# Products of the identity in two of TensorE's gaps, in a four-layer kernel

## The reference, cut to what matters

```
L0_attn: Q, K, V, gate = x @ W;  scores = (Q K^T) * decay;  Y = scores V;  normalise per head;  (silu(gate) * Y) @ W_O
L0_ffn:  y = x @ (quantised kernel + a b) + bias
L1_attn: retention in chunks of 64 tokens, 4 heads, a gate, W_o
L1_ffn:  route the top 256 of 512 tokens through gelu(x W1 + b1) W2 + b2, weighted by sigmoid(score)
```

## Time and profile before

| what | us |
|---|---|
| median of 3 runs | 806.22 |
| lowest, highest | 803.87, 809.37 |
| the profiled execution, its own time | 807.99 |
| its span, first to last instruction | 805.8 |
| TensorE busy in the span | 757.8 (94%) |
| VectorE, ScalarE, GpSimd busy | 665.8, 424.5, 475.3 |
| mean granted clock of TensorE | 0.977 |

### The profile page before, as it was taken

One profiled execution on the slowest core, in us unless ns is written; L12 is line 12 of the kernel. 1 busy time (PEld: TensorE's weight loads), 2 busy tenths in 40 slices (PEclk: granted clock), 3 DMA queues, 4 the chain that ended last, 5 costly groups with the idle time before them and its releaser, 6 DMA issues.

```text
span 805.8 us, 29577 instructions
## 1 busy us (share of the span) xinstructions
PE 757.8 (94%) x13001; PEld 614.8 (76%) x13001; DVE 665.8 (83%) x1825; ACT 424.5 (53%) x875; POOL 475.3 (59%) x375
## 2 busy tenths in 40 slices
PE   5778999999999999998999999999999999999875
PEld 4666888787887787776878888877888888878653
DVE  6686888888888999997858889987777988888887
ACT  2333555565555565654554446655544565564745
POOL 4467888887888888876543444444434344453544
PEclk9996999999999999999999999999999999999988
DMA  7000100011111110010000000000000000000113
GB/s 229 30 28 29 29 28 16 16 28 29 29 28 30 28 29 2 3 55 3 1 2 2 3 3 2 2 2 2 3 2 2 3 2 2 3 2 16 55 39 105
DMA packets 23284, 18.57 MB, mean 23 GB/s; under 512 B 2146, under 2 KB 20468, under 8 KB 22900
## 3 DMA queue, kind: packets, MB, share of 16 engines
q1 hardware_dynamic: 22596, 16.40, 7.0%
q10 hardware_dynamic: 560, 0.28, 0.1%
HBM read 12.48 MB, written 4.19 MB: 21 GB/s over the span
## 4 chain that ended last, share of the span: by engine, by line
PE 75%; DVE 17%; POOL 3%; ACT 2%; issue 1%; DMA 0%; DVEq 0%; POOLq 0%; ACTq 0%
PE ps L286 20%; PE ps L410 11%; PE ps L401 10%; PE ps L281 5%; PE ps L675 4%; PE ps L364 3%; PE ps L308 3%; PE ps L297 3%; PE ps L384 3%; PE ps L394 2%; POOL grstd L1067 2%; PE ps L356 2%; DVE x L1225 2%; PE ps L667 2%; PE ps L320 2%; PE ps L685 2%
## 5 line engine op out<-in xcount | busy, mean ns | idle before, releaser
L1067 POOL TENSOR_TENSOR grstd<-gve,mhalf 128x32 f32<-128x32 f32 (+1 forms) x32 | 159.0, 4968 | 26.5 <-DVE gve L1280 26.5
L410 PEld LDWEIGHTS ps<-w_s,hid 128*128 128x128 f32 x1024 | 123.5, 192 | 9.0 <-issue 8.0
L410 PE MATMUL ps<-w_s,hid 128*128 128x128 f32 x1024 | 129.0, 277 | 0.7 <-issue 0.7
L401 PE MATMUL ps<-xt_r,w_s 128*128 128x512 f32 x256 | 126.7, 617 | 0.7 <-ACT xt_r L822 0.7
L826 ACT ACTIVATE hid<-ps,b_s 128x512 f32<-128x512 f32 x128 | 84.0, 726 | 24.0 <-PE ps L401 23.8
L1063 POOL TENSOR_TENSOR r_ret<-ve_ret,powers 128x8 f32<-128x8 f32 x32 | 57.8, 1807 | 27.6 <-DVE ve_ret L1211 27.6
L286 PE MATMUL ps<-w_qkvg,xt_p 128*128 128x128 f32 x512 | 71.2, 285 | 2.8 <-ACT xt_p L822 2.8
L1073 POOL TENSOR_TENSOR um<-um 128x96 f32<-128x96 f32 (+1 forms) x32 | 21.3, 665 | 88.5 <-DVE um L1259 88.5
L401 PEld LDWEIGHTS ps<-xt_r,w_s 128*128 128x128 f32 x256 | 45.2, 192 | 35.1 <-issue 30.1
L1058 POOL TENSOR_TENSOR rstd_ln_mod<-ve_ln_mod,mhalf 128x4 f32<-128x4 f32 x32 | 32.3, 1010 | 65.3 <-DVE ve_ln_mod L1211 65.3
L1253 DVE TENSOR_TENSOR sc<-ps,tri 128x1024 f32<-128x1024 f32 (+1 forms) x64 | 58.3, 953 | 15.1 <-PE ps L320 7.6
(11 more groups left out here) (236 smaller groups left out, 1749.8 us busy)
## 6 DMA issues: line engine op xcount, KB each, us to landing
xtin<-in_xt SPq DMA_DIRECT2D x16, 256.0 KB, 3.8
out_x<-base SPq DMA_DIRECT2D x16, 256.0 KB, 2.3
xin<-in_x SPq DMA_DIRECT2D x15, 256.0 KB, 3.0
rot<-in_rot SPq DMA_DIRECT2D x2, 1024.0 KB, 5.9
w_s<-in_w SPq DMA_DIRECT2D x2, 256.0 KB
xin<-in_x ACTq DMA_DIRECT2D x1, 256.0 KB, 4.0
w_qkvg<-in_wqkvg SPq DMA_DIRECT2D x1, 256.0 KB, 3.8
w_qkv<-in_wqkv SPq DMA_DIRECT2D x1, 256.0 KB
```

What stands on the lines that cost most here:

```text
L401: nc.tensor.matmul(bank(k), w1_s[:, f, :], xt["r"][:].rearrange("p j n -> p (j n)"), start=True, stop=True).then_inc(s[f"h{f}"], 1)
L410: mm = nc.tensor.matmul(bank(k, j * P, P), hid[:, f, j * P:(j + 1) * P], w2_s[:, f, :], start=False, stop=(f == last and j == NT - 1), ski ...
L1067: nc.gpsimd.tensor_tensor(grstd[:, 0:n], gve[:, 0:n], mhalf[:, 0:n], ALU.pow) \
```

## The change

A helper `keep_busy(times, k)` issues `times` products of the identity with itself into bank k. It is called in two places of TensorE's program: five products into bank 2 in slot g = -1, behind the gate product of batch 0 and ahead of the wait for `qkr`; and 18 products into bank 6 (X1) in `slot_end`, behind `transpose_y` and ahead of the wait for `ln_mod_xn`. One line is indented further, inside the same `if`. No wait or signal is added or removed.

```diff
+            def keep_busy(times, k):
+                for _ in range(times):
+                    nc.tensor.matmul(bank(k, 0, P), ident, ident, start=True, stop=True)
+
...
                 if g < 0:
-                    centre_first()
+                        centre_first()
...
                     routed_up(2, up[2])
+                if g < 0:
+                    keep_busy(5, 2)
                 if sl.prepare and not route:
                     wait(pe, "qkr", new)
                     wait(pe, "v", new)
...
                 rank_sum(3, 1, 1)
                 transpose_y(now)
+                keep_busy(18, X1)
                 wait(pe, "ln_mod_xn", old)
                 wait(pe, "ystore", sl.count(-2))
                 transpose4("ln_mod", h, X2)
```

## The result

| | median of 19 runs, us | lowest to highest |
|---|---|---|
| before | 806.42 | 803.73 to 811.56 |
| changed | 803.41 | 799.70 to 806.88 |

The ratio is 0.9962, interval [0.9947, 0.9977]: 3.0 us less, within 1%. The forecast was 805.1, so the time lies in the range, but the gain is near three times the one forecast. The range, 801.6 to 807.8, holds no change as well.

What follows compares the result with a forecast made beforehand. It took the chain of waits as the bound, TensorE holding 75% and VectorE 17%. The end's 1.1 us and 0 for the five, taken from the median 806.22, gave 805.1, range 801.6 to 807.8.

Steps and rivals of the forecast that it cites:

- The fit of the 18: Last slot's gap behind `transpose_y`: 18 products at 0.24 us take 4.3, end at 767.4 before `h` at 767.99, cost 0.
- The walk through the end: Last slot from `h` at 768.0 to `x2`: with the clock held high, `output_b` starts 1.15 us earlier, taken as 1.1.
- VectorE as the new releaser of `transpose_gated`: Last slot: `transpose_gated` waits for VectorE's gated product, done at 771.73, no longer for TensorE; starts at 771.8, 1.3 us earlier.
- the limit by `rankb`: Last slot: `rank_sum(3, 3)` waits for VectorE's `rankb` at 773.03, which does not move; third hidden product starts at about 773.15.
- the unchanged lengths behind `x2`: After `output_b`, the output product, VectorE's threshold and `x2` keep their lengths; the later 0.76 us wait for `h` moves with `x2`.
- Rival 1: Last slot: the clock falls anyway near 769.4; only 0.4 us gained, 805.8, or 806.2 if the products did nothing; chance 15%.
- Rival 2: Last slot: filler products over 0.27 us each hold up TensorE's queue; slower, 807.8 or 808.9 us; chance 6%.
- end term: Last slot: a held clock gains 1.1 us, with bounds 0 and 1.3, the profiled clock returning at 772.8.
- Rival 3: Low stretch longer in other executions: 2.7 us gained at the end, 803.5; up to 1.3 near the start, 802.2; chance 20%.
- The term of the five: Near the start, before the wait on `qkr`: five products hidden at cost 0, fall at 21.9 stays, gain 0, at most 0.5.
- The reason given for the range: TensorE's low-clock stretch from 64 to 72, untouched by the change, is worth 2.8 us where it appears or not.

## Why the prediction was right and where it failed

The time fell into a range that had been made wide for the scatter of three runs; that says little about the gain, of which the forecast had a good third.

**The fit of the 18** was right: 4.18 us where I took 4.3, cost 0, and the clock held. **The walk through the end** was right in each step: VectorE as the new releaser of `transpose_gated`, the limit by `rankb`, the unchanged lengths behind `x2`. It gave 1.15, taken as 1.1, and this pair of profiles 1.28. Rival 1 (the clock falls anyway) occurred in none of the seven profiles with the 18 or the 36 transposes in the gap. Rival 2's point, 0.27 a product, was not reached: 0.23.

**The size of the end term** was too small for the typical execution: 1.1 against 1.5 by the runs, 1.8 by the profiles. The level's return at 772.8 was a property of that execution and not of the program, and it was early. Rival 3 said so and got 20%.

**The term of the five** failed: "I expect the fall at 21.9 to stay, and take 0", with an upper bound of 0.5. The runs give 1.5, more than half of what was missing. Two things were left out of the term. It priced one place of the fall: that one does stay, in both profiles with only the five, but where it comes at 24 the five take it away, with the slow scores and the next fall. And it asked only about the clock: the queue's stop within slot 0's attention products, 0.39 us in the profiled execution and 0.5 to 0.7 on the way to the next state products, never occurs with the five. How the 1.5 divides between the two isn't shown, since no run has the one without the other.

So 1.5 + 1.5 = 3.0 stands against 1.1 + 0. Rival 3, whose two halves I had worked out as 1.6 more at the end and up to 1.3 at the start, names both places and the clock's part, not the queue's. The rule cited there from the Trainium skill (TensorE: Matmul & The Clock Gate, "The HAM clock gate"; the gate's timing runs free of the kernel's start) was borne out: the kernel before gave 9.96 and 11.13 in two profiles, and its low stretch from 62 on lasted 14 and 7 us. It should have moved the forecast. The reason given for the range was right in kind: that low stretch was there in every execution whose gaps were not filled, but its length varied, and the longer form costs 2.7.

**Left open**: what stops TensorE's queue. In the last slot it did in six of 14 profiles, five times with the same three products left of the 64 (with 13 left in the changed kernel), for 0.53 to 0.91, and `h` paid 0.84 to 1.22. Five of the seven profiles without products near the start have this stop, one of the seven with them, so the five may also act here. Products behind TensorE's last instruction changed neither stop. A hint, not tested: ahead of 12 of the 13 groups that stopped a short transfer (16 GB/s over a window of 1 us) begins 0.5 to 1.0 us before the group's start, and of the 15 that did not stop ahead of none; the page of the profile before lists 102 packets of the instruction queue with 1.67 MB, so 16 KB each. A control that moves TensorE's instructions without touching the clock would settle it.

## What to carry to other kernels

Where one engine's clock depends on its recent work, a single profile shows one draw: take at least two of the kernel before, and price a term that depends on the clock as a mean over where the fall could lie, not where it lay. Unread work that fits into a gap ahead of a wait costs nothing as long as it ends before the awaited operand; count it from the rows and leave a margin. Once one gap pays, try them all: two fillings gave 3.0 us, eleven gave 6.7 and took most of the scatter with them. And an addition can act otherwise than by what it was made for: compare the two traces mark by mark behind it, and not only the clock.

## What the runs showed that I had not expected

- 36 transposes of the identity held the clock at 1.00 as 18 products did, at the same cost (4.09 and 4.18).
- Most of the run-to-run scatter of the kernel before (801.35 to 808.57 in 29 runs of the last series) goes with the gaps: 798.43 to 798.96 in 6 runs with all of them filled and three products before 13 us. With only the five, whose profiles show no stop of the queue, it stays (801.24 to 806.96), so it is mainly the clock's.
- TensorE's queue can stop for 0.39 to 1.09 us within a dense run of small products, and on the path it costs more than its own length: 0.53 to 0.91 cost 0.84 to 1.22 in the last slot. Near the start five products ahead of it went with its absence in seven profiles of seven.
